# Attention plus routed experts on one core: stores of two lead-in tiles on ScalarE's queue, two value tiles inside the attention loop, tiles ordered second half first

## What is computed

```python
# x: (1, 4096, 256), 16 heads of 16
q, k, v = (lora(x, W, A, B) for W, A, B in (Wq..., Wk..., Wv...))   # x @ W.T + x @ B.T @ A.T * 2
s = q @ k.T / 4 + slope[h] * (i - j);  s = where(j <= i, s, -1e30)  # causal, a slope for each head
x = layernorm(x + softmax(s) @ v @ Wp.T)
probs = softmax(x @ Wg);  top 2 of 8 experts, capacity 1076 tokens each
x = layernorm(x + sum over the 2 of gate * (gelu(x @ W1[e] + b1[e]) @ W2[e] + b2[e]))
```

## Time and profile before

| | us |
|---|---|
| median of 3 runs | 1244.25 |
| the three runs | 1242.29, 1244.36, 1244.25 |
| the profiled execution, its own time | 1242.23 |
| span of the trace of the profiled execution | 1240.3 |
| PE busy | 1158.9 (93%) |
| ScalarE busy | 905.6 (73%) |
| VectorE busy | 632.1 (51%) |

### The profile page before, as it was taken

One profiled execution on the slowest core, in us unless ns is written; L12 is line 12 of the kernel. 1 busy time (PEld: TensorE's weight loads), 2 busy tenths in 40 slices (PEclk: granted clock), 3 DMA queues, 4 the chain that ended last, 5 costly groups with the idle time before them and its releaser, 6 DMA issues. The chain is left out here.

```text
span 1240.3 us, 24570 instructions
## 1 busy us (share of the span) xinstructions
PE 1158.9 (93%) x8775; PEld 509.3 (41%) x8776; DVE 632.1 (51%) x1794; ACT 905.6 (73%) x1189; POOL 351.8 (28%) x391
## 2 busy tenths in 40 slices
PE   8999999999999999999999989699999999999980
PEld 4322222222222222222222111277687787787770
DVE  4544333232356435734453302548767768768746
ACT  2789999999999999999999989344435435435314
POOL 5421211111123121231213120023453552552440
PEclk9999999999999999999999989799999999999995
DMA  5843232322321322133220101444433523421226
GB/s 166 183 112 73 85 82 67 83 66 90 85 71 57 107 57 69 50 105 86 44 74 32 45 15 27 160 129 114 114 48 103 132 25 111 123 31 14 28 23 271
DMA packets 84098, 104.09 MB, mean 84 GB/s; under 512 B 15415, under 2 KB 69308, under 8 KB 83984
## 3 DMA queue, kind: packets, MB, share of 16 engines
q1 hardware_dynamic: 67128, 77.33, 21.9%
q0 software_dynamic: 15968, 24.12, 9.4%
q10 hardware_dynamic: 888, 1.16, 0.3%
HBM read 56.88 MB, written 47.96 MB: 85 GB/s over the span
## 5 line engine op out<-in xcount | busy, mean ns | idle before, releaser
L1484 ACT ACTIVATE prob<-ps_s 128x1024 f32<-128x1024 f32 (+4 forms) x841 | 705.8, 999 | 45.5 <-PE ps_s L1375 44.6
L1392 PE MATMUL ps_o<-prob,v_aug 128*17 128x512 f32 (+3 forms) x3236 | 422.5, 568 | 3.6 <-DVE acc L1564 2.8
L1375 PE MATMUL ps_s<-qop,kop 51*128 51x512 f16 (+3 forms) x1618 | 259.9, 369 | 19.8 <-ACT prob L1484 8.3
L1375 PEld LDWEIGHTS ps_s<-qop,kop 51*128 51x128 f16 x1618 | 62.3, 93 | 386.2 <-ACT prob L1484 368.0
L2418 PE MATMUL ps_y<-w2s,hs 128*128 128x256 bf16 (+1 forms) x1728 | 189.1, 273 | 0.6 <-DVE yb L2504 0.6
L2399 PE MATMUL ps_h<-xs,w1s 128*128 128x384 bf16 (+1 forms) x1152 | 179.9, 315 | 5.2 <-ACT hid L2466 4.5
L2466 ACT ACTIVATE hid<-ps_h,b 128x384 f32<-128x384 f32 (+1 forms) x192 | 105.0, 559 | 108.5 <-PE ps_h L2399 84.5
L1564 DVE COPY acc<-ps_o 32x512 f32<-32x512 f32 (+2 forms) x108 | 74.2, 687 | 192.9 <-PE ps_o L1392 191.5
L2418 PEld LDWEIGHTS ps_y<-w2s,hs 128*128 128x128 bf16 (+1 forms) x1728 | 157.7, 99 | 17.5 <-DVE yb L2504 0.7
L2355 POOL DMA_INDIRECT result<-y,entry x72 | 111.6, 1550 | 174.8 <-DVE y L2509 140.3
L1520 POOL TENSOR_SCALAR_AFFINE_SELECT prob<-prob 128x256 f32<-128x256 f32 (+1 forms) x179 | 69.1, 398 | 317.8 <-ACT prob L1484 315.8
(11 more groups left out here) (204 smaller groups left out, 760.5 us busy)
## 6 DMA issues: line engine op xcount, KB each, us to landing
w<-in_W SPq DMA_DIRECT2D x16, 1024.0 KB, 7.5
slots_x<-empty POOLq DMA_DIRECT2D x12, 520.0 KB, 4.2
qop<-fparts_q SPq DMA_DIRECT2D x42, 128.0 KB, 4.6
xe<-slots_x SPq DMA_DIRECT2D x8, 650.0 KB
aT<-attnT SPq DMA_DIRECT2D x16, 256.0 KB
x_all<-in_x SPq DMA_DIRECT2D x8, 512.0 KB
result<-x_all SPq DMA_DIRECT2D x8, 512.0 KB, 3.4
x_all<-result SPq DMA_DIRECT2D x8, 512.0 KB, 6.5
```

Of the source, the lines that this page charges most:

```text
L1375: mm = pe.matmul(ps_s[:, u.p % SLOTS_S, e, a.q0:], o.key(e, a.h, a.kt), o.query(e, a.h, a.b, a.q0), start=True, stop=True)
L1392: mm = pe.matmul(ps_o[32 * c:32 * c + VW, a.q0:], o.v[:, a.kt, a.h], prob[:, t % RING, c % 2, c // 2, a.q0:], start=a.first, stop=a.last)
L1484: act.activation(prob[:, t % RING, n, e:z, q0:], ps_s[:, u.p % SLOTS_S, e:z, q0:], ACT.Exp, scale=1.0 / (SCALE * SCALE)).then_inc(exp_done, 1)
```

## The change

Five things are edited together. (1) `TILE_ORDER` becomes (3, 1, 2, 0): second half of keys, second half of queries, first half of keys, first half of queries. SP stores only the first two tiles of block 0 and goes on to `load_first` of both halves. (2) ScalarE's queue stores the third and the fourth tile of block 0, with a part of the bias between them (`store_bias_early`) and the rest behind them. (3) Only two value tiles of block 0 stand in the lead-in, one to a bank, copied out by VectorE; the other two are pieces of turns 0 and 2. The eight warming matmuls are gone. (4) In place of all eight low parts, the first unit waits for six and the second for eight. (5) VectorE starts the bias chain one place earlier, and the norm of block 0 moves from turn 1 to turn 4; the pieces up to turn 32 move two turns back, and the keys of blocks 2 to 7 are loaded after piece (2, 1) where it was (1, 1), since the key tile is now third.

```diff
-TILE_ORDER = (3, 2, 1, 0)
+TILE_ORDER = (3, 1, 2, 0)
...
-HALF_AT = {2: (14, 16, 18, 20, 22, 24, 26, 28),
+HALF_AT = {2: (16, 18, 20, 22, 24, 26, 28, 30),
-NORM_AT = {0: 1, 1: 12, 2: 30, 3: 68, 4: 115, 5: 168, 6: 235, 7: 305}
-VALUE_AT = {1: (4, 6, 8, 10),
-            2: (32, 34, 38, 42),
+NORM_AT = {0: 4, 1: 14, 2: 32, 3: 68, 4: 115, 5: 168, 6: 235, 7: 305}
+VALUE_AT = {0: (0, 2),
+            1: (6, 8, 10, 12),
+            2: (34, 36, 38, 42),
...
-        if _p[2:] == (1, 1):
+        if _p[2:] == (2, 1):
             KEYS_AT[_t + 3] = _p[1]
...
+    def store_bias_early(j, act):
+        act.wait_ge(j.bias_step, 7)
+        a, z = j.between(1)
+        act.dma_start(j.bias.rearrange("c h a t -> (c h) a t")[a:z], j.bias_h[a:z]).then_inc(j.bias_moved, 16)
     def store_bias_first(j, act):
-        act.wait_ge(j.bias_step, 7)
         for h, to in (SWAPPED, SWAPPED[::-1]):
             act.dma_start(j.bias[:, to], j.bias_h[h:P:H]).then_inc(j.bias_first, 16)
-        for c in range(2):
+        (only c = 0)
...
         if m == 1:
-            sp.wait_ge(j.bias_first, 16 * 4)
+            sp.wait_ge(j.bias_moved, 16 * 4)
+        else:
+            sp.wait_ge(j.bias_first, 16 * 3)
... (sync)
-                for k in range(3):
+                for k in range(2):
                     j.store(sp, 0, k)
                 j.load_first(sp, 1)
-                j.store(sp, 0, 3)
                 j.load_first(sp, 0)
... (tensor)
-                for s in range(KT):
-                    if s >= 2:
-                        pe.wait_ge(j.v_out, 2 * (s - 1))
-                    j.pe_value(pe, 0, s, banks(4 + s % 2)[:, 0:D + E])
-                j.pe_warm(pe, 8, ps_r)
+                for s in range(2):
+                    j.pe_value(pe, 0, s, banks(4 + s)[:, 0:D + E])
                 pe.wait_ge(j.small_loaded, 16 * 2)
-                pe.wait_ge(j.tail_done, 8)
...
+                    if u.p < 2:
+                        pe.wait_ge(j.tail_done, 4 + 2 * u.p + 2)
                     if u.p == 2:
-                        pe.wait_ge(j.v_out, 2 * KT)
+                        pe.wait_ge(j.v_out, 2 * 2)
... (scalar)
                     if n == 0:
+                        j.store(act, 0, 2)
+                        j.store_bias_early(act)
+                        j.store(act, 0, 3)
                         j.store_bias_first(act)
-                for s in range(KT):
-                    j.act_value(act, 0, s, banks(4 + s % 2))
...
                     if t == 2:
                         act.wait_ge(j.bias_out, 16 * (NB - 1))
+                        act.wait_ge(j.bias_first, 16 * 3)
... (vector)
                 bias = j.dve_bias(dve)
+                next(bias)
                 j.dve_less(dve, 0, banks(0))
                 next(bias)
                 j.dve_tail(dve, 0, 0, banks(0))
                 next(bias)
-                j.dve_less(dve, 1, banks(1))
+                j.dve_tail(dve, 0, 1, banks(1))
                 next(bias)
-                for k in range(1, 4):
-                    j.dve_tail(dve, 0, k, banks(k))
-                    next(bias)
+                j.dve_less(dve, 2, banks(2))
+                next(bias)
+                j.dve_tail(dve, 0, 2, banks(2))
                 for _ in bias:
                     pass
+                j.dve_tail(dve, 0, 3, banks(3))
                 j.dve_weights(dve, 2, banks)
                 for k in range(4):
                     j.dve_tail(dve, 1, k, banks(k))
+                for s in range(2):
+                    j.dve_value(dve, 0, s, banks(4 + s))
```

More of the change, by code:

```diff
@@ L245 @@
     PIECE_AT[NORM_AT[_n]] = ("norm", _n)
+    PIECE_AT.update({t: ("value", _n, s) for s, t in enumerate(VALUE_AT[_n], 0 if _n else 2)})
     if _n >= 1:
-        PIECE_AT.update({t: ("value", _n, s) for s, t in enumerate(VALUE_AT[_n])})
         assert VALUE_AT[_n][-1] <= DIAG_TURN[_n] - 3
@@ L252 @@
         assert sorted(_turns) == list(_turns) and max(VALUE_AT[_n - 1][-1], NORM_AT[_n - 1]) < _turns[0]
-assert NORM_AT[0] < VALUE_AT[1][0] < NORM_AT[1] and VALUE_AT[1][-1] < HALF_AT[2][0]
+assert VALUE_AT[0][1] < NORM_AT[0] < VALUE_AT[1][0] < NORM_AT[1] and VALUE_AT[1][-1] < HALF_AT[2][0]
+assert VALUE_AT[0][0] < VALUE_AT[0][1] <= 2 + LAG and NORM_AT[0] <= 3 + LAG
 for _n in range(NB - 1):
@@ L256 @@
     PIECE_AT[COUNT_AT[_n]] = ("count", _n)
-assert len(PIECE_AT) == 2 + 8 * (NB - 2) + NB + 4 * (NB - 1) + 5 * (NB - 1) and BOUND_TURN > NORM_AT[NB - 1] + 1
+assert len(PIECE_AT) == 2 + 8 * (NB - 2) + NB + 4 * (NB - 1) + 2 + 5 * (NB - 1) and BOUND_TURN > NORM_AT[NB - 1] + 1
 SPLIT_W_AT = {2: 0, 4: 1, 6: 2, 8: 3}
@@ L275 @@
             assert _t + 8 <= FIRST_TURN[_p[1]]
-    if _p[0] == "value" and _p[2] == KT - 1 and _p[1] + 2 < NB:
+    if _p[0] == "value" and _p[2] == KT - 1 and 1 <= _p[1] < NB - 2:
         X_AT[_t + 1] = _p[1] + 2
@@ L555, in __init__ @@
         j.sets = sem("sets")
-        j.bias_in_loaded = sem("bias_in_loaded")
+        j.bias_moved = sem("bias_moved")
         j.bias_step = sem("bias_step")
@@ L569, in load_weights @@
         for a in range(3):
-            sp.dma_start(j.bias_in[:, a], io["key_const"][:, a].rearrange("h (c t) -> c h t", c=NB)).then_inc(j.bias_in_loaded, 16)
+            sp.dma_start(j.bias_in[:, a], io["key_const"][:, a].rearrange("h (c t) -> c h t", c=NB)).then_inc(j.bias_moved, 16)
         j.load_weight(sp, 2, j.w_loaded)
@@ L603, in between @@
         return max(0, H * (c - 1) + max(SWAPPED) + 1), min(P, H * c + min(SWAPPED))
+    def store_bias_early(j, act):
+        act.wait_ge(j.bias_step, 7)
+        a, z = j.between(1)
+        act.dma_start(j.bias.rearrange("c h a t -> (c h) a t")[a:z], j.bias_h[a:z]).then_inc(j.bias_moved, 16)
     def store_bias_first(j, act):
-        act.wait_ge(j.bias_step, 7)
-        rows = j.bias.rearrange("c h a t -> (c h) a t")
         for h, to in (SWAPPED, SWAPPED[::-1]):
             act.dma_start(j.bias[:, to], j.bias_h[h:P:H]).then_inc(j.bias_first, 16)
-        for c in range(2):
-            a, z = j.between(c)
-            act.dma_start(rows[a:z], j.bias_h[a:z]).then_inc(j.bias_first, 16)
+        a, z = j.between(0)
+        act.dma_start(j.bias.rearrange("c h a t -> (c h) a t")[a:z], j.bias_h[a:z]).then_inc(j.bias_first, 16)
     def load_first(j, sp, m):
@@ L706, in act_head @@
         if m >= 2:
-            act.wait_ge(j.less_set, 2 * (k + 1))
+            act.wait_ge(j.less_set, 2 * (k // 2 + 1))
         act.activation(j.part[:, m, 0, :], bank, ACT.Identity, bias=j.less[:, m - 2] if m >= 2 else 0.0).then_inc(j.head_done, 1)
[L710 to L713, removed]
     def dve_sets(j, dve):
@@ L724, in dve_bias @@
         c = Chain(dve, j.bias_step, 0, 7)
-        dve.wait_ge(j.bias_in_loaded, 16 * 3)
+        dve.wait_ge(j.bias_moved, 16 * 3)
         f, h = j.bias_f, j.bias_h
@@ L764, in dve_less @@
         dve.tensor_reduce(less, bank[:, 0:ANCHOR], AX.X, ALU.add).then_inc(j.less_set, 1)
-        dve.wait_ge(j.less_set, 2 * k + 1)
+        dve.wait_ge(j.less_set, 2 * (k // 2) + 1)
         dve.tensor_scalar(less, less, -1.0 / ANCHOR, None, ALU.mult).then_inc(j.less_set, 1)
@@ L1347, in _ @@
                 pe.wait_ge(j.weff_done, 2)
-                for k in range(2):
-                    j.pe_tile(pe, 0, k, banks(k))
+                j.pe_tile(pe, 0, 0, banks(0))
                 pe.wait_ge(j.weff_done, 4)
-                for k in range(2, 4):
+                for k in range(1, 4):
                     j.pe_tile(pe, 0, k, banks(k))
```

## The result

The changed kernel ran in 1235.45 us (median of four runs, 1234.91 to 1239.85) beside 1243.58 us for the kernel before: ratio 0.9943, interval 0.9925 to 0.996, so by the ratio 7.1 us faster, within 5.0 to 9.3 (the two medians lie 8.1 apart). The forecast was 1237.3 in a range of 1234.0 to 1241.0. Two more series of the same kernel gave ratios of 0.9961 (0.9947 to 0.9974) and 0.9937 (0.9922 to 0.9952). By the medians the three series give 8.1, 4.5 and 7.6 us. All 16 runs together have a median of 1237.6 against 1243.4 for the 69 runs of the kernel before in all series: **5.8 us**; against the 32 runs of it in these three series alone (1243.9) it is 6.4. Forecast: 6.9.

What follows compares the result with a forecast made beforehand. The lead-in was taken as held by a chain of queued DMAs that left PE idle, then cold; attention had little room. 8.2 - 1.2 - 0.1 = 6.9 us gained, from median 1244.25 to 1237.3, range 1234.0 to 1241.0.

Steps and rivals of the forecast that it cites:

- PE's first 26 us and what is removed behind them: Lead-in: PE's work to 26.04 us stays, 8.45 us behind it goes; turn 0 starts 8.2 us earlier, bounds 5.0 and 8.45.
- ScalarE's ten DMAs cost nothing: Lead-in, between the two blocks' heads: ten DMAs take 5.1 us, from 17.1 to 22.6, covered by PE's tiles.
- First loads land near 24.3, margin 1.7 us: SP's queue in the lead-in: last loads of load_first(1) leave at 21.9 and land near 24.3, before PE's 26.04.
- 1.2 us for the two pieces in turns 0 to 3: Two value tiles placed inside the first turns cost PE 1.2 us, between 0.3 and 2.2.
- 0.1 us for VectorE: Turns 4 and 5: the norm's work ahead of the first copy-out delays PE by 0.1 us; bounds 0 and 1.
- The rest costs nothing: Pieces up to turn 32 slide two turns and keys of blocks 2 to 7 load later, at no cost.
- A: Transfers bound the turns behind the lead-in; block 1's loads late for turn 14: 1 to 3 us lost, chance 0.18.
- B: Lead-in: first loads land 2 to 4 us after 26.04, leaving a gain of 3 to 5 us; chance 0.10.
- C: Turn 0 entered at low clock after a long wait for first loads, without warming: about 1247 us, chance 0.04.
- D: Last head of block 1 still waits for a landing, behind ScalarE's DMAs: gain 4 or 5 us, chance 0.05.

Runs made afterwards that it cites:

- e0: The changed kernel run again with no edit, second series: 1238.39 us (1235.04 to 1240.32, six runs), ratio 0.9961.
- e13: The changed kernel run once more with no edit, third series: 1236.64 us (1234.38 to 1238.66), with 1244.23 for the kernel before.
- e2: The changed kernel with the third and fourth tile of block 0 stored by SP again, the fourth behind load_first(1): 1242.67 us, ratio 0.9989.
- e3: The changed kernel with one more fp32 tile product (1.78 us of PE, result unused) between the two value tiles and turn 0: 1238.54 us.
- e10: The changed kernel with one half tile of block 6 moved from turn 204 to 206: 1236.62 us (1234.48 to 1237.92).
- e11: The kernel before with the same half tile of block 6 moved from turn 204 to 206: 1242.52 us, ratio 0.9993.
- e8: e10 with turn 0 also waiting for the first half of block 0's keys and queries: 1242.25 us, ratio 0.999.
- e7: e10 with tiles in the old order (3, 2, 1, 0), SP storing the first and third, ScalarE the others: 1236.21 us (1234.46 to 1241.36).
- e1: The changed kernel with all four value tiles of block 0 back in the lead-in, without warming: 1238.77 us, ratio 0.9962.

## Why the prediction was right, step by step

**PE's first 26 us and what is removed behind them.** Right in what is removed: from the start of the tiles to the first score it was 25.48 us and is 17.70 in e0 and 17.31 in e13. e2 shows the cause of the head's wait to be the one named (4.09 us with the two stores back on SP). It also shows that this wait no longer holds the first score, only unit 1, and that most of its price, about 4 of 5.8 us, is clock. Two parts of the change were not tried alone: the warming matmuls taken out, and six low parts in place of eight for unit 0.

**ScalarE's ten DMAs cost nothing.** Right, with less room than laid out. They left between 16.90 and 23.04 us in e0 (17.1 to 22.6 forecast), and e0 had begun its tiles 0.46 us early, so the last left 0.9 us later than laid out. Heads ran from 23.22 and the last low part ended at 26.55 (26.2 forecast). Unit 0 was not held up; unit 1's weights waited 0.26 us for it.

**First loads land near 24.3, margin 1.7 us.** Wrong. They left SP when forecast (21.7 against 21.9) and landed 1.9 us later, near 26.2. The step that failed is the allowance of 2.4 us for a landing; the prediction's own had a median of 4.1 for the queries' loads, and 2.4 is next to their least. It hurt little: PE was busy to 25.58 in e0 and 26.42 in e13 anyway, and waited 0.67 and 0.28 us. That the first score, forecast for 26.3, came at 26.25 in e0 is partly luck, since tiles that began 0.46 us early made up for the wait; in e13 it came at 26.70. The Trainium skill (page "DMA: Bandwidth & Descriptors", section "Issuing engines are not separate DMA queues") says that queues of different engines run on the same 16 DMA engines and that a second one only saves time of the issuing sequencer. This case agrees with the first half in so far as loads landed later where more was under way (4.5 us after issue in e0, 1.9 in e2). What the change of queue saved was not so much the 0.42 us of an issue as the wait ahead of it.

**1.2 us for the two pieces in turns 0 to 3.** Right, forecast a little too high. In e0, e3, e10 and e13 alike turn 4 begins 0.93 us later relative to turn 0 than it did.

**0.1 us for VectorE.** Right. In the profiled execution the copy-out ends at 38.75 and the value product that needs it starts at 39.21, straight behind the piece. Up to turn 305 both terms together cost 1.3 us (e3) or 1.2 (e10 against e11), 1.3 forecast.

**The rest costs nothing.** By the code's own waits, right. But the prediction took one thing as given: that 800 us of later work keep their length when they start earlier. They do, except for the clock. The 1.93 us hole near 400 us was in the trace of before and looked harmless there. All three profiled executions of the changed kernel had 3.4 us of half clock behind it, 1.5 us each. Without that drop and the one near 10 us (8.83 - 7.13 = 1.7 us), the way from the start of the tiles to the norm of turn 305 is 6.5 us (e3, less 1.0 for the added work), 6.9 us (e13) and 7.1 us (e10 against e11) shorter than it was. 6.9 was forecast. Between 1235 and 1240 lie these two drops, the start of the tiles (8.54 to 10.08 us over all traces) and the stretches behind turn 305. That is put together from executions of 1236.8 to 1239.9 us; none near 1235 was profiled. So that the medians of the series, 8.1, 4.5 and 7.6 us, lie around 6.9 shows the size, but how near a single one falls is luck.

Whether the shift made the drop at 400 us more frequent isn't settled. It is in five of six traces with this hole behind the change, and not in the one before it; e11 moved the kernel before by less than its interval, which speaks for rare there, but its runs were not profiled one by one.

**Rivals.** A was named with some 2 us of room left; that room was gone: turn 14 waited 0.53 and 0.44 us for the loads (first profile, e13), 0.2 us more than for ScalarE alone in e0. B came true in its mechanism (loads later than laid out), at under 0.7 us. C's sum was that a delay x costs x + 1.7 + 1.3 against 8.2. e8 made x 5.3 (22.46 us from the tiles to the first score; e10 has 18.83, of which 1.70 are its cold tiles), for which it gives no gain, and 0.999 was measured. But its term for the clock was too small: from the first score to turn 305 e8 needs 3.0 us more than e10 (589.81 - 31.78 = 558.0 against 555.0), not 1.7, since the low level lasted 10.2 us and not 3.5. By the traces e8 is 1.2 us slower than e11 at turn 305, which the medians (1242.25 and 1242.52) don't show. D did not happen.

## What to carry to other kernels

When an engine idles for a transfer, look first at what is queued ahead of its issue: here 4 us hung on three 0.42 us issues that stood behind another load's wait. A queue with free issue slots fixes that, but the landing times of the old trace need not hold in the new order (4.5 us here where 2.4 was allowed). And where two versions differ by 1 or 2 us, count from one named event to another in the traces, with the granted clock beside it; the medians of e3, e7 and e1 showed nothing of 1.0, 1.8 and 2.7 us that the traces showed plainly. Choose the later event ahead of places where the clock falls in every trace.

## What was not expected of the hardware

The clock may drop behind a hole of under two us in PE's work, or behind none that the busy column shows (9 to 10 us, busy 1.00). Holes of the same size did and didn't lower it: 1.78 us in e2 and 1.93 to 1.96 us in five traces did, 1.93 us in the kernel before, 1.94 in e3 and 1.86 in e7 did not. And the same program has a drop in one execution and not in the next (near 10 us in the first profile of the changed kernel, not in e0 and e13). The length of the low stretch varied more than its cause: about 3.4 us in the kernel before, behind 3.13 us of idle time and with warming matmuls in it, and about 10 us in e2 and e8, behind 1.78 and 5.42 us of waiting and with the first turns' work in it. That the warming matmuls make this difference is a guess; no run tried them alone.
